# Two-layer kernel: the last stage's routing exponential and 1/sqrt as powers on GpSimd, and routing from unit 6 of a tile

## The reference, cut to what matters

```python
x = x + _L1_ffn_ref(_layernorm(x), ...)

def _L1_ffn_ref(x, centroids, expert_biases, Ws_up, Ws_down, W_up, W_down):
    shared = silu(xf @ Ws_up) @ Ws_down
    aff = xf @ centroids.T                       # T x 64
    _, idx = top_k(aff + expert_biases, 8)
    w = sigmoid(take_along_axis(aff, idx, axis=1))
    w = w / (sum(w, axis=-1, keepdims=True) + 1e-08)
    cw = zeros((T, 64)).at[arange(T)[:, None], idx].add(w)
    h = silu(einsum('td,edf->etf', xf, W_up))    # 64 experts, F = 64
    y = einsum('etf,efd->etd', h, W_down)
    return shared + einsum('etd,te->td', y, cw)

def _layernorm(x, eps=1e-05):
    return (x - mean(x)) / sqrt(var(x) + eps)
```

## Time and profile before

| | |
|---|---|
| time, median of 3 runs | 1111.92 us (1108.44 to 1113.43) |
| span of the profiled execution, first to last instruction | 1102.4 us |
| TensorE (matmul) busy | 948.5 us, 86% of the span |
| VectorE busy | 845.6 us, 77% |
| ScalarE busy | 719.1 us, 65% |
| GpSimd busy | 446.7 us, 41% |
| mean granted TensorE clock | 0.929 of full; 1.00 in the last stage but its first microseconds |
| last stage | 659 us to the end; up matmul of unit 0 of tiles 0 to 7 at 658.90, 713.93, 768.84, 823.84, 878.81, 935.19, 990.16, 1044.63 us |

### The profile page before, as it was taken

How to read it: one execution, slowest core, us unless ns; L and a number is a source line. 1 busy time by engine, 2 the same in 40 slices (tenths; PEclk the granted TensorE clock), 3 DMA queues, 4 the chain that set the end, 5 groups by cost and what they waited for, 6 DMA issues and landing times.

```text
span 1102.4 us, 20447 instructions
## 1 busy us (share of the span) xinstructions
PE 948.5 (86%) x6019; PEld 747.6 (68%) x6052; DVE 845.6 (77%) x1938; ACT 719.1 (65%) x1416; POOL 446.7 (41%) x510
## 2 busy tenths in 40 slices
PE   4652099999658999999999979999999999999998
PEld 3541099999536677677767657676767676767676
DVE  6888177777567888888888657888787878787865
ACT  4650055555346877877777657777777778787776
POOL 1378650000156665565553403333333333333333
PEclk8655599999858999999999989999999999999999
DMA  8011122222210110100100008382838383838382
GB/s 250 26 49 61 50 57 67 63 65 66 66 32 21 30 30 23 33 25 24 35 21 20 1 7 194 71 207 62 189 80 196 73 189 74 192 77 192 79 193 72
DMA packets 63921, 89.99 MB, mean 82 GB/s; under 512 B 16559, under 2 KB 54610, under 8 KB 59730
## 3 DMA queue, kind: packets, MB, share of 16 engines
q1 hardware_dynamic: 59136, 80.33, 30.4%
q0 software_dynamic: 4096, 8.40, 2.7%
q10 hardware_dynamic: 594, 0.09, 0.0%
HBM read 70.90 MB, written 17.89 MB: 81 GB/s over the span
## 4 chain that ended last, share of the span: by engine, by line
PE 63%; DVE 12%; issue 7%; ACT 7%; POOL 7%; DMA 2%; SPq 1%; DVEq 0%; POOLq 0%; ACTq 0%
POOL xs L661 6%; PE ps L2146 4%; PE ps L2128 4%; PE ps L2130 4%; PE ps L2129 4%; PE ps L2148 4%; PE ps L2147 4%; PE ps L1932 3%; PE ps L1875 3%; PE ps L1956 3%; PE ps L1950 2%; PE ps L1995 2%; PE ps L1978 2%; PE ps L1854 2%; PE ps L1853 2%
## 5 line engine op out<-in xcount | busy, mean ns | idle before, releaser
L809 POOL TENSOR_TENSOR hl<-h,hh 128x512 fp32r<-128x512 f32 x128 | 165.6, 1294 | 292.1 <-ACT hh L1081 292.1
L1081 ACT ACTIVATE hh<-h 128x512 fp32r<-128x512 f32 (+1 forms) x264 | 165.1, 625 | 44.2 <-DVE h L1711 42.7
L1711 DVE TENSOR_TENSOR h<-ps,cwB 128x512 f32<-128x512 f32 x192 | 130.5, 680 | 45.3 <-ACT ps L1070 35.5
L1611 DVE TENSOR_REDUCE nm<-ps 128x4 f32<-128x512 f32 (+1 forms) x128 | 116.4, 951 | 35.7 <-PE ps L1978 33.8
L715 POOL DMA_INDIRECT yg<-ys,gps x64 | 63.0, 985 | 166.4 <-issue 155.9
L1070 ACT ACTIVATE ps<-ps 128x512 f32<-128x512 f32 x192 | 111.7, 582 | 26.2 <-PE ps L2130 25.6
L2146 PE MATMUL ps<-hh,wh 128*128 128x512 f32 x256 | 106.1, 414 | 11.4 <-DVE hl L1718 10.4
L2128 PE MATMUL ps<-xh,wh 128*128 128x512 f32 x256 | 105.0, 410 | 0.0
L2129 PE MATMUL ps<-xl,wh 128*128 128x512 f32 x256 | 101.6, 397 | 0.0
L2130 PE MATMUL ps<-xh,wl 128*128 128x512 f32 x256 | 101.4, 396 | 0.0
L2148 PE MATMUL ps<-hh,wl 128*128 128x512 f32 x256 | 101.3, 396 | 0.0
(11 more groups left out here) (326 smaller groups left out, 2692.3 us busy)
## 6 DMA issues: line engine op xcount, KB each, us to landing
cwB<-cwd SPq DMA_DIRECT2D x32, 1536.0 KB, 14.4
cwd<-cwS SPq DMA_DIRECT2D x64, 96.0 KB
xb<-xs SPq DMA_DIRECT2D x72, 64.0 KB, 1.8
ys<-yb SPq DMA_DIRECT2D x72, 64.0 KB, 1.6
x_res<-in_L_attn_x_dram SPq DMA_DIRECT2D x4, 512.0 KB, 6.8
wst<-in_L_ffn_W_up_dram SPq DMA_DIRECT2D x32, 64.0 KB, 2.2
wst<-in_L_ffn_W_down_dram SPq DMA_DIRECT2D x32, 64.0 KB, 1.9
out_dram<-y SPq DMA_DIRECT2D x8, 256.0 KB, 13.2
```

The source lines that it names most:

```text
L809: pool.tensor_tensor(hl4[:, slot(u), :], h4[:, slot(u), :], hh4[:, slot(u), :].bitcast(F32), op=ALU.subtract).then_inc(u_hlp, 1)
L1081: act.activation(hh4[r, slot(u), :], h4[r, slot(u), :], ACT.Copy).then_inc(u_hh, 1)
L1611: ins = dve.tensor_reduce(nm[:, u, 4 * g:4 * g + 4], o, axis=AX.X, op=ALU.max, negate=True)
L1711: dve.tensor_tensor(h4[:, slot(u), :], first, second, op=ALU.mult).then_inc(u_h, 1)
```

## The change

- Two constants are added, 1/e and -1/2, one value in each partition.
- In the last stage GpSimd takes the exponential as (1/e) to the power af, in two halves of 128x128 elements behind its `hl` of units 15 and 17 (`X4_EXP`), and the 1/sqrt as (var + eps) to the power -1/2, two instructions of 128x4 behind `hl` of unit 5. ScalarE no longer does either, and its explicit table load at unit 16 goes.
- The semaphore of the exponential now counts two for a tile; VectorE's sigmoid waits for both halves.
- Norm moves from unit 10 to 6. The transposes and their copy move from 12 to 11, the logits from 14 to 13. VectorE's steps `xh` to `chosen` move one unit earlier, to 12 to 18, sigmoid to 21, the first reciprocal to 22, times chosen to 23, sum to 24, and plus 1e-8 and the second reciprocal both to 25; the last three stay at 26, 27 and 28.

```diff
--- before.py
+++ after.py
@@ -5,6 +5,7 @@
 
 
 
+import math
 from contextlib import ExitStack
 
 import concourse.bass as bass
@@ -88,6 +89,8 @@
         x_res = sb("x_res", [P, NT, D], F32)
         ident = sb("ident", [P, P], F32)
         eps_c = sb("eps_c", [P, 1], F32)
+        inv_e = sb("inv_e", [P, 1], F32)
+        neg_half = sb("neg_half", [P, 1], F32)
         RT = 2 * SUB
         NR = NT // RT
         assert NR == 4
@@ -438,6 +441,8 @@
 
             return bank[3] if isinstance(n, int) and n == 0 else bank[6]
 
+        X4_TURN, X4_LOGITS, X4_EXP = 11, 13, 15
+
         def slot(u):
 
             return u % 4 if u else 4
@@ -620,6 +625,8 @@
             own.done(pool.memset(ident[:, :], 0.0))
             own.done(pool.memset(trif[:, :], 1.0))
             own.done(pool.memset(eps_c[:, :], LN_EPS))
+            own.done(pool.memset(inv_e[:, :], math.exp(-1.0)))
+            own.done(pool.memset(neg_half[:, :], -0.5))
             own.done(pool.memset(zrow[:, :], 0.0))
             own.done(pool.memset(bias3[0:96, :], 0.0))
             own.done(pool.memset(ones[:, :], 1.0))
@@ -802,12 +809,33 @@
 
             turns(pool_turn, pool)
 
+            def x4_rstd(n, p):
+
+                pool.wait_ge(d_mv, n + 1)
+                apart(pool, pool_passed)
+                pool.tensor_scalar(lnv[:, p, :], mv[:, p, :, 1], LN_EPS, None, ALU.add).then_inc(act_d, 1)
+                pool.wait_ge(act_d, n + 1)
+                pool.tensor_tensor(rstd[:, p, :], lnv[:, p, :], neg_half[:, :].broadcast_to([P, SUB]), op=ALU.pow).then_inc(d_rs, 1)
+
+            def x4_exp(n, k):
+
+                if k == 0:
+                    pool.wait_ge(d_afc, n + 1)
+                    apart(pool, pool_passed)
+                ins = pool.tensor_tensor(g4[:, 0, k:k + 2, :], inv_e[:, :].unsqueeze(2).broadcast_to([P, 2, E2]),
+                                         af[:, k:k + 2, :], op=ALU.pow)
+                ins.then_inc(d_ex, 1)
+
             def pool_tile(t, p, before, N, S):
                 for u in range(1, NU, 2):
                     pool.wait_ge(u_hh, t * NU + u + 1)
                     apart(pool, pool_passed)
                     pool.tensor_tensor(hl4[:, slot(u), :], h4[:, slot(u), :], hh4[:, slot(u), :].bitcast(F32),
                                        op=ALU.subtract).then_inc(u_hlp, 1)
+                    if u == 5 and S:
+                        x4_rstd(t + 2, p)
+                    if u in (X4_EXP, X4_EXP + 2) and N:
+                        x4_exp(t + 1, u - X4_EXP)
 
             tiles_of(pool, pool_tile)
 
@@ -1097,13 +1125,8 @@
                                        ACT.Copy).then_inc(c_F4, 1)
                     if u == 5 and before is not None:
                         out_copy4(before[0], before[1])
-                    if u == 12 and N:
+                    if u == X4_TURN and N:
                         x4_T(t + 1, 1 - p)
-                    if u == 16 and N:
-                        act.preload_act_table_set(TABLE)
-                        x4_exp(t + 1, 1 - p)
-                        if S:
-                            x4_rstd(t + 2, p)
                     if u == 30 and N:
                         x4_weights(t + 1, 1 - p)
 
@@ -1536,7 +1559,7 @@
 
                 def sigmoid():
 
-                    dve.wait_ge(d_ex, n + 1)
+                    dve.wait_ge(d_ex, 2 * n + 1)
                     own.done(dve.tensor_scalar(g4[:, 2, :, :], g4[:, 0, :, :], 1.0, None, ALU.add))
 
                 def then(op):
@@ -1694,7 +1717,7 @@
             turns(dve_turn, dve)
 
 
-            STEP_AT = (10, 13, 14, 15, 16, 17, 18, 19, 20, 21, 22, 23, 24, 25, 26, 27, 28)
+            STEP_AT = (6, 12, 13, 14, 15, 16, 17, 18, 21, 22, 23, 24, 25, 25, 26, 27, 28)
 
             def e_h(t, u):
                 dve.wait_ge(u_sg, t * NP2 + u)
@@ -1740,7 +1763,7 @@
                                       x_res[:, t, :], op=ALU.add).then_inc(c_F6, 1)
 
             def dve_tile(t, p, before, N, S):
-                steps = dict(zip(STEP_AT, routing(t + 1, 1 - p))) if N else {}
+                steps = list(zip(STEP_AT, routing(t + 1, 1 - p))) if N else []
                 if before is not None:
                     e_lo(before[0], NU - 1)
                 for u in range(1, NU):
@@ -1752,8 +1775,9 @@
                         x4_stats(t + 2, p)
                     if u == 9 and before is not None:
                         result(*before)
-                    if u in steps:
-                        steps[u]()
+                    for at, step in steps:
+                        if at == u:
+                            step()
 
             tiles_of(dve, dve_tile)
             e_lo(T // TT - 1, NU - 1)
@@ -2169,9 +2193,9 @@
                         last_attended(u)
                     if u == 7 and before is not None:
                         out_T(before[0])
-                    if u == 12 and N:
+                    if u == X4_TURN and N:
                         x4_turned(t + 1, t if before is not None else None)
-                    if u == 14 and N:
+                    if u == X4_LOGITS and N:
                         x4_logits(t + 1)
                     if u == 30 and N:
                         x4_weights(t + 1)
```

## The result

The changed kernel takes 1353.74 us (median of 4 runs, 1350.42 to 1356.15) against 1110.86 us for the kernel before in the same comparison (1108.44 to 1113.43): a ratio of 1.218, with a 95% interval of 1.214 to 1.221. It is 243 us slower.

A forecast was written before the change was run, and what follows sets the result against it. Routing's gaps in TensorE's last stage were the bound. Gain 5.6 - 2T, 1.8 us a tile at T = 1.9: seven tiles 12.6, plus 1 for `xm`, less 1 for arbitration; 1111.9 - 12.6 gives 1099 us, 8-in-10 range 1087 to 1124.

The forecast's parts named there:

- bound of the gaps: Last stage: TensorE's gaps, 4.07 us in the tile shown and 28 us in seven, are the ceiling of the gain.
- parity of the steps: VectorE's two sigmoid-related tensor_scalars move to odd units (21, 25), away from GpSimd's `hl`: 0.5 and 0.7 us less.
- `xm` term: Earlier norm has `xm` ready before TensorE's transposes: 0.2 us a tile in six tiles, 1 us.
- term T: Time of one GpSimd pow of 128x128 elements, behind `hl` 15 and 17: taken as 1.9 us, ends 0.46 and 3.9.
- price of a microsecond: Last stage, seven tiles: gaps of 2T - 1.5 us a tile, so one microsecond of T costs 14 us.
- an e_lo that runs through a pow: Sign at unit 16: VectorE's e_lo unhindered by the pow makes the forecast wrong; gain near B's whatever T up to 2.
- B: Rival: pow about as cheap as a subtract, T under 1.4; most gaps close, 1084 to 1092 us; chance 0.18.
- rival D: Units 16 to 23: pow over 3.2 us pushes `hl` 19 by 2(T - 1.5) and locks VectorE out; slower; chance 0.22.
- break-even: The pow length at which the change would neither gain nor lose: T = 2.8 us.
- Q: The experiments' theory, not the prediction's: pow costs its place in GpSimd's queue, with 1.5 us free in each pause.
- E: Rival: a table load stays in the tile, gaps as before with the pows on top, 1112 us or more; chance 0.01.
- new wait: Unit 16: VectorE's e_lo 16, with two SBUF inputs, waits until pow 1 ends at 854.0 + T.

The follow-up runs named there:

- tanh kernel: The changed kernel with ScalarE's tanh replacing the exponential in tiles 1 to 7 and the 128x256 reciprocal dropped there: 1084.12 us, ratio 0.976.
- moves alone: The changed kernel with exponential and 1/sqrt back on ScalarE with the table swap, all steps in their new places: 1099.19 us, ratio 0.990.
- the one with 20 elements: The changed kernel with each large pow cut to 20 elements a partition, the rest of the exponential left out: 1104.50 us, ratio 0.992.
- probe: The changed kernel with four more chained VectorE instructions on scratch tiles behind unit 20, under a running pow: 1356.48 us in one run.
- kernel with four pows: The changed kernel with the exponential in four pows of 128x64, behind `hl` 15, 17, 19 and 21, instead of two: 1363.77 us, ratio 1.228.

## Why the prediction was wrong

**The bound of the gaps was right.** 4.07 us a tile, 28 us in all, and three gaps with two causes. The tanh kernel closes them and gains 26.3 us. Without the swap and the reciprocal but with the steps in their old places, 0.77 us stay at `cs`; with the moves alone, the 1.6 us of the swap and 1.0 at `cs` stay. The parity of the steps did what the working said (0.55 and 0.66 us for the two tensor_scalars, in place of 0.5 and 0.7). What it missed is that `xh` and `chosen` moved onto even units: in the kernel with the moves alone they grew by 0.56 and 0.22 us, and in the tanh kernel `chosen` by 0.60. The `xm` term held: the 0.2 us a tile are gone.

**The step that failed is the term T in "What is added".** The prediction took 1.9 us, with 0.46 and 3.9 as ends; a pow of 128x128 elements takes 20.72 us, five times the upper end. Two rows of the changed kernel give its law: 1.04 us for 4 elements and 20.72 for 128, so 0.40 + 0.159 us an element, 70 times the 2.2 ns an element of GpSimd's tensor_tensor (0.74 us for 256, 1.29 for 512). The law gives 1.67, 3.57 and 10.56 us for 8, 20 and 64 elements; measured were 1.73, 3.53 and 10.52. The upper end was no bound: I took the ratio of 4.3 between two operations of VectorE for that between two operations of GpSimd, and doubled it. The nearest row in kind was of another engine, and said nothing about this one. An operation of which the trace has no row on the same engine leaves its price open upward, and the range should have said so.

**The price of a microsecond was right, the way was wrong.** "One microsecond of T is 14 us of the kernel", and 2T - 1.5 = 39.9 us of gaps a tile at T = 20.72, hence 1111.9 + 7 x (39.9 - 4.07) - 1 = 1362 us, against 1353.74 measured. That it comes so near is luck: the queue alone gives 37.0 us a tile, and the restarts at the lower clock, which the sum did not have, fill up half of the difference or all of it. And the sum reached this through e_lo 16 and `chosen`, which it let wait for the pows. They do not: e_lo 16 took 0.79 us under a pow in the changed kernel and 0.68 in the one with 20 elements, `chosen` (L1558 at 878.15) 0.41. The prediction had named this sign too: an e_lo that runs through a pow makes the forecast wrong, with a gain near B's for T up to 2, and at 1.73 us it was. The slope of two comes from GpSimd's queue, 2 x (T - 1.5) - 1.4, which is part of rival D. Between T of 1.4 and 3.6 the two ways give different numbers: at 1.73 us the kernel gains 24.6 us where the sum gave 15, and at 3.53 it still gains 7 where the sum gave a loss of 10. The break-even would be near 4 us of T, not at 2.8. That is an estimate, as no run lies between 3.5 and 10.5 us: by the queue the gaps at T are 2T - 4.4 plus 0.2 to 0.5 us at `cs`, and 4.07 is reached at 4.0 to 4.1.

**The 243 us by their parts**, in tile 2, by the distances of TensorE's starts less 0.23 each: the first wait 17.8 us, the restart behind it at the 1.2 GHz level 2.2, the second wait 16.9. Together they are 36.9 us, and Q has 37.0: the restart between the pows costs nothing of its own, since `hl` 19 would have been waited for in any case. The second restart adds 1.5 us (1.4 to 2.9 in the seven tiles). Less the 4.07 and 0.2 us of before, that is 34.1 us (34.0 to 35.5), and the tiles grew by 34.0 to 35.8 us (89.1 to 90.4 against 54.5 to 56.4).

**The rivals.** D, slower by a long pow, was the one that happened, with 0.22; its place (units 16 to 23) and price were as told, and its push of `hl` 19 by 2(T - 1.5) is what the runs show, but VectorE was not locked out, and its size was not imagined. E did not happen: in the last stage of the changed kernel ScalarE has one table load. A sign that speaks for D before any run was in the working itself: GpSimd has 34 us free a tile, and at more than 0.13 us an element the exponential fits nowhere. This threshold could be worked out from rows, and I did not set it beside the open price.

**The rule of the port.** The Trainium skill (SBUF — State Buffer, Who interferes with whom) has a VectorE instruction with two SBUF inputs wait for a GpSimd instruction that reads SBUF, and one in a 2-port mode for any GpSimd instruction, to its end. For GpSimd's subtraction the runs agree (tensor_scalar 1.35 us at 918.57, on top of `hl`). For its pow they do not: the probe ran through it in its free times, and e_lo 16 was held for the first 0.27 us of 20.7 and no longer. The measurement decides; the prediction's new wait, taken from the row of `xl` and this rule, was an extension to an operation that no row showed.

## What to carry to other kernels

Before an operation is handed to an engine, look for a row of that operation on that engine; without one, its price has no upper end, and the first question is at which price the idle time of the engine is used up. A function that shares the table already loaded (tanh beside silu) can take the place of one that does not, and an algebraic step that cancels may free a second engine. VectorE's steps belong where the neighbour on the shared port is idle; here the unit's parity was worth 0.5 to 0.9 us an instruction.

## What the runs showed of the hardware

GpSimd's pow, fp32, as measured: 0.40 us plus 0.159 us for each element of a partition, from 4 to 128 elements, and 20.715 to 20.732 us in 14 instructions on different data. Its multiplication of the same shape takes 0.49 us.

A running pow does not hold VectorE up: tensor_scalar of 128x256 took 0.28 us and tensor_tensor 0.42 us under it, while both wait for GpSimd's subtraction. Only its first moment does. e_lo 16, which takes 0.68 us when free, took 0.88 us when it began 0.07 us into a pow of 128 elements, 0.77 with 64, 0.70 with 20 and 0.68 with 8: held until 0.27, 0.16 and 0.09 us behind the pow's start, about 1.7 ns more for each element. That this is the time in which pow reads its input would fit, and is not shown.

ScalarE computes Tanh and Silu in turn without a table load: one load, at the start of the 414 us of the last stage, with 7 Tanh in it.

TensorE's granted clock fell to the 1.2 GHz level in each wait of about 17 us (0.50 in the 4.5 us behind the first one of tile 2) and also in the waits of 6.4 to 11.3 us in the kernel with four pows (0.50 to 0.52 behind them). The matmuls restarted at 0.43 us in place of 0.23, and a restart took 1.1 to 2.9 us longer than at the full clock. Behind the waits of 0.8 and 1.9 us in the kernel with 20 elements the granted clock was 1.00 and nothing was lost.
